# Turning attention results on VectorE instead of TensorE, with earlier row statistics and stage hand-overs

## The reference

```python
scores = einsum('bmhd,bnhd->bhmn', q, k) / sqrt(dqk)      # 8 heads, dqk = 2
scores = where(scores >= 0, scores, 0.2 * scores)
out = einsum('bhmn,bnhd->bmhd', softmax(scores), v)       # dv = 16
attention = gamma * out + xn
```

## Time and profile before

| what | us |
|---|---|
| median of 3 runs | 977.76 (976.85 to 977.84) |
| profiled execution | 976.61 |
| its span | 974.8 |
| busy in the span: PE, DVE, ACT, POOL | 883.5, 744.3, 716.5, 581.7 |
| up to the first centred tile | 28.4 |
| 16 groups of the prologue | 74.2 |
| router | 34.6 |
| attention, 12 passes | 243.8 |
| experts | 181.4 |
| attention, 20 passes, and the end | 412.4 |

### The profile page before, as it was taken

One profiled execution on the slowest core, in us unless ns is written; L12 is line 12 of the kernel. 1 busy time (PEld: TensorE's weight loads), 2 busy tenths in 40 slices (PEclk: granted clock), 3 DMA queues, 4 the chain that ended last, 5 costly groups with the idle time before them and its releaser, 6 DMA issues.

```text
span 974.8 us, 19803 instructions
## 1 busy us (share of the span) xinstructions
PE 883.5 (91%) x7619; PEld 365.8 (38%) x7620; DVE 744.3 (76%) x851; ACT 716.5 (74%) x859; POOL 581.7 (60%) x574
## 2 busy tenths in 40 slices
PE   0688249999999999999999989999999999999997
PEld 0444102333333333867767723333333333333332
DVE  6698889999999995001011089999999999999996
ACT  0689878888888887454454468888888888888886
POOL 3355137776676662999999015647566574665770
PEclk9999659999999999999999989999999999999999
DMA  8723100101100011242342210010011002002100
GB/s 228 269 65 72 31 27 30 44 30 36 39 25 28 18 52 58 68 135 92 110 135 78 80 43 26 22 49 20 26 32 39 23 21 64 24 13 62 31 7 22
DMA packets 48163, 55.34 MB, mean 57 GB/s; under 512 B 10714, under 2 KB 35122, under 8 KB 48080
## 3 DMA queue, kind: packets, MB, share of 16 engines
q1 hardware_dynamic: 38464, 44.10, 14.8%
q0 software_dynamic: 8192, 9.37, 3.3%
q10 hardware_dynamic: 1424, 0.76, 0.3%
HBM read 31.58 MB, written 30.02 MB: 63 GB/s over the span
## 4 chain that ended last, share of the span: by engine, by line
PE 77%; ACT 9%; DVE 6%; issue 4%; DMA 1%; SPq 1%; POOLq 0%; ACTq 0%; DVEq 0%
PE ps L765 26%; PE ps L745 15%; PE ps L735 13%; PE ps L825 8%; PE ps L817 8%; ACT pr L636 4%; PE ps L775 3%; ACT ot L628 2%; DVE xn L897 1%; SPq L248 1%; PE ps L695 1%; PE ps L806 1%; ACT y L614 1%; DMA y<-in_x 1%; ACT va L592 1%
## 5 line engine op out<-in xcount | busy, mean ns | idle before, releaser
L1030 DVE TENSOR_SCALAR ps<-ps 128x1024 f32<-128x1024 f32 x512 | 610.7, 1229 | 20.9 <-PE ps L735 6.6
L636 ACT ACTIVATE pr<-ps 128x1024 f32<-128x1024 f32 x512 | 523.3, 1024 | 111.5 <-PE ps L745 101.0
L765 PE MATMUL ps<-pr,vp 128*32 128x256 f32 x4096 | 327.7, 392 | 0.3
L745 PE MATMUL ps<-q,kz 64*128 64x512 bf16 x1024 | 201.7, 391 | 9.2 <-DVE ps L1030 9.1
L735 PE MATMUL ps<-q,kz 62*128 62x512 bf16 x1024 | 199.9, 387 | 7.7 <-DMA q<-parts_dram 1.7
L445 POOL DMA_INDIRECT xs<-eout,idxs x128 | 129.0, 1008 | 108.7 <-ACT pr L636 78.5
L430 POOL DMA_INDIRECT disp<-xn,idx x128 | 125.6, 981 | 47.1 <-issue 35.8
L1042 DVE TENSOR_TENSOR pr<-ps,parts 128x1024 f32<-128x1024 f32 x12 | 14.7, 1225 | 166.1 <-PE ps L825 166.1
L745 PEld LDWEIGHTS ps<-q,kz 64*128 64x128 bf16 x1024 | 49.2, 93 | 222.0 <-DVE ps L1030 117.2
L765 PEld LDWEIGHTS ps<-pr,vp 128*32 128x32 f32 x4096 | 81.2, 108 | 108.1 <-issue 91.3
L663 ACT ACTIVATE pr<-ps,b1s 128x512 f32<-128x512 f32 x96 | 66.0, 687 | 48.8 <-PE ps L817 48.8
(11 more groups left out here) (120 smaller groups left out, 618.6 us busy)
## 6 DMA issues: line engine op xcount, KB each, us to landing
disp<-pr SPq DMA_DIRECT2D x12, 512.0 KB, 4.9
eout<-pr SPq DMA_DIRECT2D x12, 512.0 KB, 2.9
y<-in_x SPq DMA_DIRECT2D x8, 512.0 KB, 8.2
out<-y SPq DMA_DIRECT2D x8, 512.0 KB
w<-in_w1t SPq DMA_DIRECT2D x12, 256.0 KB, 3.1
w<-in_w2t SPq DMA_DIRECT2D x12, 256.0 KB, 3.3
xs<-disp SPq DMA_DIRECT2D x6, 512.0 KB, 4.8
pr<-disp SPq DMA_DIRECT2D x6, 512.0 KB, 4.8
```

Of the source, the lines that this page charges most:

```text
L636: act.activation(pr[:, c % BUFS, 2 * pair:2 * pair + 2, :], ring[i % RING], ACT.Exp, scale=SLOPE).then_inc(S["exps"], 1)
L745: last = pe.matmul(ring[i % RING][:, k, :], kz[r:r + TILE, hg, pair, kc * P:(kc + 1) * P], q2[r:r + TILE, hg, qh * HALF:(qh + 1) * HALF], ...
L765: last = pe.matmul(acc[p % 2][32 * g:32 * g + 32, cols], vp[:, hg, kc, g, :], pr[:, c % BUFS, g % PAIRS * 2 + g // PAIRS, cols], start=(kc ...
L1030: dve.tensor_scalar(s, s, 0.0, 1.0 / SLOPE - 1.0, ALU.max, ALU.mult).then_inc(S["relu"], 1)
```

## The change

- **Turn.** ACT's copy and PE's four transposes inside the passes go. DVE transposes `acc` (PSUM, 128 x 512 f32) in blocks of 32 x 32 straight to `ot`, ahead of unit 5 of the next pass, and takes the reciprocals from `ot` ahead of unit 6. POOL does the multiplication (`quotient`). Each head's rows then lie on partitions 32 g to 32 g + 31 for every block of 32 queries; SP sends 16 transfers of 32 partitions x 256 bytes (`spread`) that bring them to their place in `moved`, and POOL adds `moved` to `y` one pass later. The last pass of each attention stage keeps the old way.
- **POOL's pace.** Its transfers go to units 1 to 6 and from 9 on; `value_rows`, the addition and the quotient stand between.
- **Statistics in halves.** The statistics of sequences 0 to 3 alone come ahead of the groups; those of 4 to 7 are taken at the ends of steps 0 to 3, their variance in step 3, the roots in steps 4 and 5. DVE centres groups 0 to 2 ahead of step 0 and group n + 3 in step n.
- **Hand-overs.** PE transposes expert 0's block before the last three value products of the first attention stage. ACT scales it before it copies `acc`, and PE turns `acc` between the second and third product of expert 0. The first two scores of the second attention stage are issued in the middle of the last expert's second product, and DVE does their leaky part before the last bias addition. ACT waits for the last product where it waited for the last store, and for the store only at unit 6. ACT loads its function tables ahead of need (`ready`).
- **Last sequence.** It is stored in two halves. The first pair of experts is taken out of the loop.

```diff
+            def spread(p):
+
+                sp.wait_ge(S["att_rdy"], quotients(p))
+                wait_done(sp, "y_att", p - 1)
+                for g in range(HG):
+                    for r in range(NR):
+                        sp.dma_start(moved[BLOCK * r:BLOCK * r + BLOCK, p % 2, g, :, :],
+                                     att[BLOCK * g:BLOCK * g + BLOCK, p % 2, r, :, :]).then_inc(S[f"spread{p % 2}"], 16)
+
+            def operands_in(p):
+
+                if p % NPB == 0 and p > 0:
+                    load_operands(p // NPB, 1)
+                if p % NPB == NQ and p // NPB + 1 < B:
+                    load_operands(p // NPB + 1, 0)
+
+            for hg in range(NHG):
+                load_operands(0, hg)
+            for p in range(BH * NPB):
+                operands_in(p)
+                if 0 < p < BH * NPB - 1:
+                    spread(p - 1)
...
+            spread(BH * NPB - 2)
...
+            def quotient(p):
+
+                pool.wait_ge(S["rg_rdy"], p + 1)
+                if p > 1:
+                    wait_done(pool, f"spread{p % 2}", 16 * HG * NR * spreads(p - 2))
+                rows = ot[:, p % 2, :].rearrange("p (t r c) -> p t r c", r=NR, c=BLOCK)[:, :, :, 0:DV]
+                inv_rows = rg[:, p % 2, :].rearrange("p (t r) -> p t r", r=NR).unsqueeze(3)
+                pool.tensor_tensor(att[:, p % 2, :, :, :].rearrange("p r t d -> p t r d"), rows,
+                                   inv_rows.broadcast_to([P, GT, NR, DV]), ALU.mult).then_inc(S["att_rdy"], 1)
...
+                early = j < (count + 1) // 2
+                unit = 1 + j * EARLY // ((count + 1) // 2) if early else (
+                    LATE + (j - (count + 1) // 2) * (UP - 1 - LATE) // max(count // 2, 1))
+                pool.wait_ge(S["exps"], UP * p + unit)
...
+                    def results():
+
+                        if p % NPB == 0:
+                            value_rows(b, 1)
+                        if p % NPB == NQ and b + 1 < B:
+                            value_rows(b + 1, 0)
+                        if p > first + 1:
+                            settle(p - 2)
+                        if p > first:
+                            quotient(p - 1)
+
+                    move(p, results)
...
-                    if i % UP == EVAC and i > first + UP:
-                        evacuate(i // UP - 1)
...
+                        act.wait_ge(S["fc2"], E_MLP)
+                    if i == BH * NUB + (BUFS - 1) * PAIRS:
                         act.wait_ge(S["yo_out"], ONE + 16 * E_MLP)
...
+            def ready(function):
+
+                act.activation(kmax[:], gam[:], function, scale=0.0)
+
+            act.wait_ge(S["pv"], BH * NPB * TB - 1)
             take_turned(0)
+            evacuate(BH * NPB - 1)
+            ready(ACT.Gelu)
...
+            ready(ACT.Exp)
             attention(BH, B)
+            evacuate(B * NPB - 1)
...
-                    if 0 <= i % UP - TURN < GT and i > first + UP:
-                        turn(i // UP - 1, i % UP - TURN)
...
+                if b1 == BH:
+                    pe.wait_ge(S["exps"], end - RING + 1)
+                    turn_rows(0, 0)
...
-                        pe.wait_ge(S["att_rdy"], NPB * BH)
+                    if n == 2 and first:
+                        turn(BH * NPB - 1)
...
+                    if half == 1 and last:
+                        ahead(BH)
...
+            ahead(0)
+            attention(0, BH)
+            for u in range(2):
+                expert(u, u, first=u == 0)
...
+            def row_stats(b):
+
                 dve.wait_ge(S[f"x_in{b}"], 16)
                 for t in range(TB):
                     last = dve.bn_stats(bst[:, b * TB + t, :], y[:, b * TB + t, :])
-            link(last)
+                last.then_inc(stat, 1)
+                step[0] += 1
...
+            for b in range(B // 2):
+                row_stats(b)
+            variance(0)
+            first_norm(0)
...
+                if at(0) and at(0)[2] + LEAD < 2 * B:
+                    centre(at(0)[2] + LEAD)
...
+            def later_rows(n):
+
+                def work():
+                    row_stats(B // 2 + n)
+                    if n == B // 2 - 1:
+                        variance(1)
+                return work
+
+            for n in range(LEAD):
+                centre(n)
+            groups(prologue, {**{n: later_rows(n) for n in range(B // 2)},
+                              B // 2: lambda: first_norm(1), B // 2 + 1: lambda: second_norm(1),
+                              2 * B: first_choice, 2 * B + 2: second_value, 2 * B + 3: second_choice})
...
+            def turn(p):
+
+                dve.wait_ge(S["pv"], TB * (p + 1))
+                if p > 1:
+                    dve.wait_ge(S["att_rdy"], quotients(p - 2))
+                dve.transpose(ot[:, p % 2, :], acc[p % 2]).then_inc(S["turned"], 1)
 
             def denominators(p):
 
-                dve.wait_ge(S["o_rdy"], p + 1)
-                dve.reciprocal(rg[:], turned(p)[:, :, :, DV]).then_inc(S["rg_rdy"], 1)
+                dve.wait_ge(S["turned"], p + 1)
+                rows = ot[:, p % 2, :].rearrange("p (q c) -> p q c", c=BLOCK)
+                dve.reciprocal(rg[:, p % 2, :], rows[:, :, DV]).then_inc(S["rg_rdy"], 1)
...
+                    if i % UP == TURN and i > first + UP:
+                        turn(i // UP - 1)
+                    if i % UP == TURN + 1 and i > first + UP:
+                        denominators(i // UP - 1)
+                    rectify(i)
...
+            expert_rows(E_MLP - 2, 0)
+            for i in range(BH * NUB, BH * NUB + AHEAD):
+                rectify(i)
+            expert_rows(E_MLP - 1, 1)
+            attention(BH, B, AHEAD)
```

More of the change, by code:

```diff
@@ L48 @@
 TAKEN = 1
+EARLY = 6
+LATE = 9
 NQ = M // HALF
@@ L239, in unit_of, with quotients, spreads @@
             return p, p // NQ % NHG, p % NQ, n // PAIRS, n % PAIRS
+        LAST = (BH * NPB - 1, B * NPB - 1)
+        def quotients(p):
+            return sum(k not in LAST for k in range(p + 1))
+        def spreads(p):
+            return sum(k not in LAST and k % 2 == p % 2 for k in range(p + 1))
         def pass_at(b, hg, qh):
@@ L473, in gather @@
                     fetch(g, p, j, len(mine))
                     if g > 0 and not new:
-                        combine(g - 1, max(p - 1, BH * NPB))
+                        combine(g - 1)
                     if g == NG - 1:
-                        combine(g, max(p - 1, BH * NPB))
+                        combine(g)
+                if len(mine) == 1:
+                    results()
             def attention(b0, b1, move):
-                for p in range(b0 * NPB, b1 * NPB):
+                first, last = b0 * NPB, b1 * NPB - 1
@@ L481, in attention @@
+                for p in range(first, last + 1):
                     b = p // NPB
[L482 to L488, removed]
-                settle(b1 * NPB - 1)
+                    def results():
[8 more added lines that the diff above has]
+                    move(p, results)
@@ L616, in residual @@
                 last.then_inc(S["y_upd"], 1)
-            groups(prologue, {**{2 * B + b: lambda b=b: residual(b) for b in range(B - 3)}})
+            groups(prologue, {B // 2 - 1: lambda: root(2, rstd, s4), B // 2: lambda: root(3, r2, s5),
+                              **{2 * B + b: lambda b=b: residual(b) for b in range(B - 3)}})
             expert_exponentials()
@@ L770, in values, with ahead @@
                     last.then_inc(S["pv"], 1)
-            def turn(p, t):
-                if t == 0:
-                    pe.wait_ge(S["acc_evac"], p + 1)
-                last = pe.transpose(acc[p % 2][:, t * P:(t + 1) * P], ot[:, p % 2, t * P:(t + 1) * P], ident)
-                if t == GT - 1:
-                    last.then_inc(S["o_rdy"], 1)
+            def turn(p):
+                pe.wait_ge(S["acc_evac"], 1 + LAST.index(p))
+                for t in range(GT):
+                    last = pe.transpose(acc[p % 2][:, t * P:(t + 1) * P], ot[:, p % 2, t * P:(t + 1) * P], ident)
+                last.then_inc(S["o_rdy"], 1)
+            def ahead(b):
+                for i in range(b * NUB, b * NUB + AHEAD):
+                    scores(i)
             def attention(b0, b1):
                 first, end = b0 * NUB, b1 * NUB
-                for i in range(first, first + AHEAD):
-                    scores(i)
                 for i in range(first, end):
@@ L856, in _ @@
             dve.sem_inc(S["comb"], CO0)
-            for b in range(B):
+            def row_stats(b):
                 dve.wait_ge(S[f"x_in{b}"], 16)
@@ L1020, in attention @@
-            def attention(b0, b1):
-                first, end = b0 * NUB, b1 * NUB
-                for i in range(first, end):
-                    done = i // UP - 1 if i > first + UP else None
-                    if done is not None and i % UP == DENOM:
-                        denominators(done)
-                    if done is not None and i % UP == FINISH:
```

(18 more changed lines are left out.)

205 lines of the change are left out of this document (112 added, 93 removed).

## The result

| | before | after |
|---|---|---|
| median of the runs | 977.8 (976.85 to 978.0, 4 runs) | 954.03 (951.2 to 955.41, 4 runs) |
| ratio | | 0.9755 [0.9731, 0.9779] |
| profiled execution | 976.61 | 953.4 |
| its span | 974.8 | 951.6 |

A forecast was written before the change was run, and what follows sets the result against it. The chain of waits, nearly all through PE at 20.08 us a pass, was taken as the bound. Gains 18.9 + 2.2 + 3.2 + 0 + 0.4 = 24.7 from 976.6 gave 951.9, plus 1.15 to the median: 953.0, range 944 to 964.

The forecast's parts named there:

- Part 1: Attention passes: moving the turn to DVE removes 0.88 us, costs 0.25; gain 0.63 in each of 30 passes, 18.9 us.
- free room of 0.6: Attention passes: a DVE stall is free up to about 0.6 us; beyond that each us costs a us.
- three shares: Attention passes: PE ahead of need 0.29, DVE idle per pair of units 0.14, PE's wait for ACT 0.18.
- estimate of 1.24 us: DVE's transpose: skill's 311 ns per 128 x 128 bf16 square, four in a row; weighed less than the 0.68 row.
- Both rivals that rested on a dear transpose: DVE's transpose costs 1.13 us (total 968 to 971, chance 0.09) or 2.26 us (total 1003, chance 0.05).
- The third, a late quotient: Ahead of unit 5, DVE waits for the late quotient or its 16 transfers; total about 971, chance 0.02.
- The first rival: DVE's transpose costs 1.13 us like a leaky part; passes gain 3, the rest 5.8; 968, up to 971; chance 0.09.
- Parts 2, 3 and 5: Gains of 2.2 us into the experts, 3.2 into the second attention stage, 0.4 at the end.
- bounds of 2.1 and 4.3: Into the second stage: range of the 3.2 us gain, since a falling clock could take some 2.2.
- Part 4: Prologue: statistics in halves gain 0; bounds were 4.4 gained if the store doesn't hold, or 2 more cost.
- not before 39.6: Prologue: zero stores are issued until 34.68 and take 4.9 to land, so nothing behind them happens before 39.6.
- both cost nothing: Attention passes: POOL's quotient (over 3 us spare) and SP's 16 issues (some 4 us) add no time.

The follow-up runs named there:

- e5: Changed kernel with DVE's transpose in two halves ahead of units 5 and 8 and the reciprocals ahead of unit 10: 950.24 us.
- e6: Changed kernel with DVE transposing only 32 of 512 columns and taking reciprocals of ones, leaving out most of the turn: 949.3 us, one execution.
- e4: Changed kernel with DVE's transpose done twice, one after the other with a wait between: 975.85 us, one execution.
- e2: Changed kernel with the 12 zero stores issued one by one behind the stores of groups 0 to 11: 946.99 us.
- e7: Changed kernel with POOL's transfers paced evenly over each pass and value rows, addition and quotient at the pass's end: 963.93 us.
- e9: Changed kernel with zero stores behind the stores of groups 0 to 11, transpose halved, reciprocals ahead of unit 10: 1084.34 us on the second chip.

## Why the prediction was right

**Part 1** was right in its mechanism: the turn leaves PE's path, DVE's stall is free up to a room, and what is beyond the room is paid. Two of its terms were off and cancelled each other. The old turn cost 0.78 a pass (20.04 - 19.26) and not 0.88, since the pass is 20.04 on the average where one of 20.08 was read, and the floor is 19.26 where the working had 19.20. The new one costs 0.17 over the floor and not 0.25: transpose 0.63 (0.60 taken), reciprocals 0.15 (0.25), stall 0.78 (0.85). So the gain is 0.61 a pass for 0.63, closer than its terms, by luck. The working's free room of 0.6 agrees with the runs (0.78 - 0.17 = 0.61): e5 and e6 show that less than the room is free, and e4 that what is added beyond is paid in full. The three shares from which the room was added up (0.29, 0.14 and 0.18) were not tested one by one.

The estimate of 1.24 us from the Trainium skill, VectorE: DVE Perf Modes, The three transpose paths, does not hold for this instruction: 706 ns. Short squares times four overstate one long instruction: 32 columns take 206 ns (e6), 256 take 427 to 440 (e5) and 512 take 706, which is about 1.04 ns a column and, as an estimate, 0.17 us that each instruction pays once. Both rivals that rested on a dear transpose fell with the estimate. The third, a late quotient, fell in its form: no DVE transpose waits for POOL. The first rival's 968 leaves out the 1.15 us that the forecast adds to come from the profiled execution to the median; with them it is 969.

**Parts 2, 3 and 5.** PE stands idle for 0.52 between the last values and the first product; undoing the hand-over costs 1.8, 2.2 was predicted. Into the second stage 2.4 of 3.2, inside the bounds of 2.1 and 4.3 that the clock had been given: it fell for 3.4 us in this trace and not at all in those of e2 and e5. The end gave 0.9 for 0.4.

**Part 4** was predicted by the queue and not by what the edit is for, and that held to a third of a microsecond: the third cast "not before 39.6", measured 39.87. That centring three groups ahead saves nothing by itself is true only while the stores hold; without them it may be worth up to 1.4.

**What was mis-sized.** "SP gets 16 issues per pass, at 0.26 each, some 4 us" was wrong by a factor of 2.6. All 480 of them (least, median and most of one issue in ns, then the first and the last start):

```profile
L333 SPq DMA_DIRECT2D moved<-att x480: 507/591/1863, 175.5 to 945.2; - x160
```

Sixteen take 10.9 us, 56% of a pass. The row of 0.26 in the earlier trace rows was of another transfer, 2 KB of `q`. The sum did not feel it: in the middle of a stage only POOL waits for these transfers (its additions four times between 640 and 900, 8.5 us in all), and POOL has 0% of the chain. But "both cost nothing" holds only for the middle: e7 shows 10 us at the two ends, e5 gives 2 us back there, and the changed kernel avoids it by where it puts the quotient.

## What to carry to other kernels

Before an engine takes over work that another did on the critical path, count how much stall it can take between two of its due times; under that room the work was free here, and work above it could be split so that each piece stayed under it. A queue for which nobody on the critical path waits in the steady state can still set the end of a stage, so follow the last round of transfers to the last store. And when an engine starts earlier and the end of the stretch does not move, look for the store that waits in a queue behind bulk stores which nobody needs yet: the gain of 4 us appeared only when both were changed.

## What the runs showed of the hardware

DVE's f32 transpose from PSUM to SBUF in blocks of 32 x 32 takes 706 ns for 128 x 512, 427 to 440 for 128 x 256 and 206 for 128 x 32: about 1.04 ns per further column ((706 - 206) / 480). The leaky part (1225 ns for 1024 columns) comes to the same, an estimate with the same 0.17 us once per instruction ((1225 - 172) / 1024 = 1.03). So going through the blocks costs nothing extra per column.

The issue of one transfer of 32 partitions x 256 bytes between SBUF tiles took SP 0.51 us or more, against 0.43 for the load of a whole 512 KB block (`xs<-disp`, e7) and 0.26 in the earlier trace rows. A zero store of 512 KB took 0.43 alone (at 32.58 in e2) and 1.07 in a row of twelve (12.79 / 12, changed kernel). The bytes do not set the price of an issue; what does, no run here shows.

The same kernel took 977.8 us on one chip and 1088.3 on another. On the second, DVE and ACT started late inside the attention passes (DVE by 2.7 us in the lines of e9), and PE was idle for 98.6 of 680 us there (5.7 of 581 in the changed kernel on the first chip). The granted clock then fell to the lower level in stretches of 3.4 to 13.7 us: at 240.1 in e9, for one, after PE had stood idle for 3.32 us up to 239.6. What makes the engines start late there is open; no run was made on it.
